# A second buffer for the expert weights that are split into two parts, with the static order of all engines planned anew

## The reference, cut to what matters

```python
xn = _layernorm(x)
# attention: q, k, v = silu(conv4(xn @ W)); delta rule in chunks of 32 steps:
#   att = (I + strict_lower(kb @ k.T))^-1 ; u = att @ v ; w = att @ kb
#   per chunk: u_adj = u - w @ S ; o = q @ S + local @ u_adj ; S += k.T @ u_adj
#   o = gated mix(short FIR, long FIR, o, v) ; rmsnorm ; @ W_o
# experts: top 2 of 8, for each chosen expert e (H=128, F=256):
x1 = xn @ W1[e] + b1[e];  x2 = xn @ W2[e] + b2[e];  z = x1 * x2
g = z @ Wg[e] + bg[e];    l = z @ Wl[e] + bl[e]
y = (silu(g) * l) @ W3[e] + b3[e];   out += weight * y
```

## Time and profile before

| | |
|---|---|
| median of 3 runs (lowest to highest) | 886.43 us (883.74 to 887.36) |
| the profiled execution | 884.17 us, its span 882.4 us |
| busy: PE, DVE, POOL, ACT | 658.0, 568.8, 458.6, 299.6 us |
| mean granted TensorE clock | 0.842 |
| moved by DMA | 64.92 MB, 74 GB/s in the mean |

### The profile page before, as it was taken

The page is one execution under the profiler, slowest core; times in us unless marked ns, Lnnn a source line. Parts: engine busy times, 40 slices in busy tenths (PEclk is TensorE's granted clock), DMA queues, the critical chain, the costliest instruction groups (busy, mean ns, idle before and its releaser), DMA issues.

```text
span 882.4 us, 31011 instructions
## 1 busy us (share of the span) xinstructions
PE 658.0 (75%) x13276; PEld 502.2 (57%) x13276; DVE 568.8 (64%) x1233; ACT 299.6 (34%) x519; POOL 458.6 (52%) x519
## 2 busy tenths in 40 slices
PE   2434856877687878878898686978878788899772
PEld 2223845666465656566666555666566646676651
DVE  6888957536747865965577546864477748533573
ACT  2221024323343425342254334333433343334230
POOL 3730168634826754676475755387435662723323
PEclk9985567989887968997899898898889798999775
DMA  7221121323113214131332204131324311310350
GB/s 290 107 96 54 61 54 39 105 64 86 26 39 78 64 32 114 39 77 53 88 108 64 77 14 108 44 92 38 54 61 74 69 38 45 93 53 31 107 196 12
DMA packets 62488, 64.92 MB, mean 74 GB/s; under 512 B 39824, under 2 KB 47888, under 8 KB 62224
## 3 DMA queue, kind: packets, MB, share of 16 engines
q1 hardware_dynamic: 54880, 46.84, 17.8%
q0 software_dynamic: 5888, 12.07, 6.1%
q10 hardware_dynamic: 1584, 4.04, 1.2%
HBM read 45.35 MB, written 17.56 MB: 71 GB/s over the span
## 4 chain that ended last, share of the span: by engine, by line
PE 29%; issue 21%; POOL 20%; DVE 18%; DMA 6%; ACT 3%; SPq 3%; DVEq 0%; POOLq 0%; ACTq 0%
PE ps_shared L1629 5%; PE ps_shared L1850 4%; POOL y_d L1042 4%; POOL xs L1031 3%; PE ps_g L1625 3%; PE ps_l L1625 3%; PE ps_x L1625 3%; DVE acc L1392 3%; PE ps_shared L1767 3%; POOL sumsq L996 2%; SPq L881 2%; DMA system_d<-masked 2%; DVE solve_prod L1466 2%; PE ps_shared L1625 2%; POOL ssq_o L1068 2%
## 5 line engine op out<-in xcount | busy, mean ns | idle before, releaser
L1042 POOL DMA_INDIRECT y_d<-work,put_i x92 | 92.3, 1004 | 80.5 <-DVE work L1605 57.4
L1031 POOL DMA_INDIRECT xs<-xn_d,owner_i x92 | 94.7, 1030 | 60.2 <-issue 24.6
L1625 PE MATMUL ps_x<-xr,w_up 128*128 128x512 f32 x276 | 98.4, 476 | 17.9 <-issue 12.0
L1076 POOL TENSOR_TENSOR z<-work,z 128x512 fp32r<-128x512 f32 x46 | 60.4, 1314 | 59.5 <-ACT z L1246 59.3
L1625 PE MATMUL ps_g<-z,w_mid 128*128 128x512 f32 x276 | 83.2, 441 | 4.6 <-POOL z L1076 4.2
L1625 PE MATMUL ps_l<-z,w_mid 128*128 128x512 f32 x276 | 82.2, 436 | 1.7 <-issue 1.1
L1392 DVE SCALAR_TENSOR_TENSOR acc<-pre,late_sb,acc 128x512 f32<-128x512 f32 x72 | 59.9, 832 | 26.9 <-ACT acc L1139 25.6
L1625 PEld LDWEIGHTS ps_x<-xr,w_up 128*128 128x128 f32 x276 | 54.8, 218 | 36.5 <-issue 18.9
L1850 PE MATMUL ps_shared<-w_plain,work 128*128 128x128 f32 x368 | 58.2, 323 | 18.1 <-DVE work L1600 13.3
L1466 DVE TENSOR_TENSOR solve_prod<-solve_T,solve_L 128x1 f32<-128x1 f32 (+14 forms) x120 | 49.4, 412 | 28.7 <-DMA solve_L<-system_d 25.3
L1850 PEld LDWEIGHTS ps_shared<-w_plain,work 128*128 128x128 f32 x368 | 53.9, 232 | 22.6 <-issue 16.5
(11 more groups left out here) (252 smaller groups left out, 1420.7 us busy)
## 6 DMA issues: line engine op xcount, KB each, us to landing
w_split<-expert_split SPq DMA_DIRECT2D x23, 768.0 KB
w_plain<-expert_plain SPq DMA_DIRECT2D x23, 196.0 KB
xa_d<-xr SPq DMA_DIRECT2D x8, 512.0 KB, 2.6
xa<-xa_d SPq DMA_DIRECT2D x8, 512.0 KB, 4.0
system_d<-masked SPq DMA_DIRECT2D x8, 256.0 KB, 2.9
x_res<-hidden SPq DMA_DIRECT2D x8, 256.0 KB, 2.8
xs<-xn_d,owner_i POOLq DMA_INDIRECT x92
y_d<-work,put_i POOLq DMA_INDIRECT x92
```

Source lines behind the costliest of these rows:

```text
L1031: pool.indirect_dma_start(xs[par][:, c, :], None, xn_d.rearrange("w p (c d) -> (w p c) d", c=CPW), bass.IndirectOffsetOnAxis(owner_i[:, w ...
L1042: pool.indirect_dma_start(y_d, bass.IndirectOffsetOnAxis(put_i[:, w * CPW + c:w * CPW + c + 1], 0), y_sb[par][:, c * D:(c + 1) * D], None) ...
L1076: pool.tensor_tensor(low[:, :], up1[i], high[:, :].bitcast(FP), ALU.subtract).then_inc(S["z_low"], 1)
L1625: made = pe.matmul(to, weights[a], x[b], start=start and n == 0, stop=stop and n == 2)
```

## The change

1. `w_split` becomes a list of two buffers, used by the tile's parity. `load_split` of tile t waits for the splits of tile t-2, and the landing is counted on one semaphore per buffer (`in_split0`, `in_split1`).
2. The planner's stream `expert_weights` becomes two, one per parity, with the same rule.
3. The descriptor part of SBUF is set to 8 KB per partition, which frees 8 KB; the second buffer takes 6 KB.
4. `PULL` and `LEAN` get other values for many of their names, so all five queues stand in another order. The instructions themselves are the same: 23 loads of 768 KB, the same splits, products and table loads.

```diff
-PULL = {"beta_T": -200, "blend": -600, "choose": 400, "combine": -250, "conv0": 50, "count": -200, "delta_T": 50,
+PULL = {"blend": -600, "choose": 400, "combine": -250, "conv0": 50, "count": -200, "delta_T": 50, "delta_again": 350,
...
-    def expert_weights():
+    def expert_weights(par):
         yield need(("place", 0, 0))
-        for t in range(TILES):
-            if t:
-                yield need(("split_up", t - 1, 0), ("split_mid", t - 1, 0))
+        for t in range(par, TILES, 2):
+            if t >= 2:
+                yield need(("split_up", t - 2, 0), ("split_mid", t - 2, 0))
             yield "load_split", t, 0, None
...
-        w_split = sb("w_split", P, SPLIT)
+        w_split = [sb(f"w_split{n}", P, SPLIT) for n in range(2)]
...
-                    if w:
-                        sp.wait_ge(S["up_low"], w)
-                        sp.wait_ge(S["mid_low"], w)
+                    if w >= 2:
+                        sp.wait_ge(S["up_low"], w - 1)
+                        sp.wait_ge(S["mid_low"], w - 1)
                     row = sp.value_load(row_i[0:1, w:w + 1], min_val=0, max_val=(EXPERTS - 1) * P)
-                    sp.dma_start(w_split[:, :], expert_split[bass.ds(row, P), :]).then_inc(S["in_split"], 16)
+                    sp.dma_start(w_split[par][:, :], expert_split[bass.ds(row, P), :]).then_inc(S[f"in_split{par}"], 16)
...
-                    act.wait_ge(S["in_split"], 16 * (w + 1))
+                    act.wait_ge(S[f"in_split{par}"], 16 * loads(w, 2))
...
-    nc = bacc.Bacc("TRN2", target_bir_lowering=False, num_devices=1)
+    nc = bacc.Bacc("TRN2", target_bir_lowering=False, num_devices=1, dynamic_dma_scratch_size=8192)
```

More of the change, by code:

```diff
@@ L122 @@
-LEAN = {"beta": -30, "beta_T": 45, "blend": 45, "combine": -15, "conv": -30, "delta_again": -40, "fetch": -10,
[L123 to L129, removed]
+PULL = {"blend": -600, "choose": 400, "combine": -250, "conv0": 50, "count": -200, "delta_T": 50, "delta_again": 350,
+        "diag": -100, "down": 200, "fir": -350, "fir_l": -600, "fir_l_T": 600, "fir_l_half": 200, "fir_s_T": -50,
+        "fold": -250, "full": 300, "fuse": -50, "fuse2": -400, "gate": 50, "gate_T": -500, "gates": 300, "gelu": 100,
+        "give": -600, "inv": 100, "inverse_out": 150, "k_T": -600, "ln": -150, "load_split": 200, "load_x": -350,
+        "load_xs": -200, "load_xt": 50, "low": 250, "masks0": -300, "mid_g": 150, "mid_l": -300, "mix_v": -350,
+        "normed": 100, "o": 50, "o_T_out": -100, "on_state": -300, "out": 50, "own": 300, "owned": 600, "place": -200,
+        "products": -250, "project": 250, "q_T": -300, "rank": -150, "solve_in": -200, "solve_mul": -50,
+        "solve_sum": -350, "split": -100, "split_mid": 550, "split_qkv": 300, "split_up": 200, "store": -600,
+        "sumsq": -300, "swish": 300, "system": 500, "times": 50, "turn": -100, "u": -150, "u_adj": 600, "u_out": -150,
+        "up1": -50, "up2": 600, "v_T": -200, "v_again": -150, "w_T_out": 400, "x_res": 150, "y_put": -600, "z": -50,
+        "zeros": 100}
@@ new lines @@
+LEAN = {"beta": -30, "beta_T": 45, "blend": 45, "combine": -15, "conv": -30, "delta_again": -40, "fetch": -10,
+        "fir": -5, "fir_l_T": -25, "fir_s_T": -25, "full": 15, "fuse": -20, "fuse2": 40, "give": -20, "inv": -20,
+        "inverse_out": -20, "k_T": 25, "ln": -40, "load_xs": -5.2, "low": 25, "mark": -15, "masks": -45, "mid_g": 12.1,
+        "mid_l": -15.6, "mix_s": -5, "mix_v": 25, "norm": -35, "o": -15, "o_T_out": -25, "owned": 10, "products": 45,
+        "project": 20, "rank": 30, "rms": -5, "silu": 5, "solve_in": -15, "solve_mul": 30, "split_mid": -13.9,
+        "state": 15, "store": 45, "sumsq": -15, "system": -10, "times": 10.4, "turn": -7.7, "u_adj": 25, "u_out": -15,
+        "up2": -3.4, "v_T": 40, "v_again": -40, "v_again_T": 15, "v_b": -60, "y_out": -8.7, "y_put": -10.4,
+        "zlow": -15.6}
@@ L526, in schedule @@
                windows(triangles), windows(attend), *(expert_loads("load_xs", n, lambda t: ("turn", WINDOWS + t, 0)) for n in range(2)),
-               *(expert_loads("load_plain", n, lambda t: ("y_out", t, 0)) for n in range(2)), expert_weights(),
+               *(expert_loads("load_plain", n, lambda t: ("y_out", t, 0)) for n in range(2)), expert_weights(0), expert_weights(1),
                expert_splits("split_up", 2, "up2"), expert_splits("split_mid", 1, "mid_l"), expert_turns(), expert_ups(), expert_zs(), expert_mids(), expert_gates(), expert_downs(), expert_puts(0), expert_puts(1),
@@ L616 @@
 SIGNALS += [f"in_xa{n}" for n in range(3)]
-SIGNALS += [f"{k}{n}" for k in ("in_xa_d", "in_plain", "in_xs", "in_y_d") for n in range(2)]
+SIGNALS += [f"{k}{n}" for k in ("in_xa_d", "in_split", "in_plain", "in_xs", "in_y_d") for n in range(2)]
 SIGNALS += [f"in_y{n}" for n in range(WINDOWS)]
```

12 lines of the change are left out of this document (6 added, 6 removed).

## The result

The changed kernel takes 901.21 us (median of 3, 898.25 to 905.45) against 886.43: a ratio of 1.0178, 95% interval 1.0104 to 1.0252. Timed again beside later experiments it came out at 1.0121 (1.0066 to 1.0177). So it is slower by 1 to 2%, where the prediction gave 879.7 and a range of 865 to 894. The profiled execution took 905.45 us, 21.3 us of span above the one of before.

The account below looks back on a forecast made before the run. PE's queue was taken to set the pace, its 136 us of standing still being what counts. Pauses -8.54, `down` +5.6, `u_adj` -2.0 and last stage -1.8 gave -6.7: 877.4 profiled, 879.7 us as median, range 865 to 894.

Parts of the forecast that it names:

- Three pauses, -8.54: PE's pauses at window 4's `low`, a window 1 state copy and window 2's `u_out` go: 4.22, 2.05, 2.27 us.
- pause 1: At `low` of window 4, PE stood 4.22 us because `parts` queued behind two `w_split` loads on SP; it goes.
- ACT waits under 10 us, SP's wait far below 245.7: Profile signs: behind 120 us ACT's `w_split` waits total under 10 us; SP's wait for splits far under 245.7.
- `down`, +5.6: PE's wait for DVE's last gate before `down`: nine more short covers at 0.62 us each, +5.6 us.
- The rival that added nine at 2.2: Nine more `down` places cost their mean price, 2.2 us each, 19.8 us together: 893.9 us; chance 0.19.
- The tail, -1.8: Last stage: window 6's `o_T` and `out` leave PE's path to the end; -1.8 us, bounds 0 and -1.8.
- `products` to `low`, 0: PE work covering the triangular solve shrinks in windows 3 and 7, DVE's foreign work too; 0, bounds -5 and +8.
- Descriptors, 0: Smaller descriptor part of SBUF: at most 9 POOL calls in flight, none stretched; 0 us.
- The other sign of being wrong: The prediction would be wrong if PE's idle time between 120 and 830 us did not fall.
- The pauses come back elsewhere: No-change rival: SP's queue still holds loads behind a `w_plain` load waiting for `y_out`; 884 to 888 us, chance 0.24.
- the calls' case: POOL's indirect calls wait for a place in the smaller descriptor ring; chance 0.03.
- the last rival: Order gains more: all 16.4 us of POOL's waits and 4.9 of `u_adj`; 860 us, 868 half way; chance 0.13.

Follow-up runs that it names:

- e6_sp: Kernel before with two w_split buffers, its order kept except in SP's queue: 20 loads of w_split and window 4's parts moved ahead; 1.0029.
- e9_up1: Kernel before with one number of PULL changed that has nothing to do with loads, up1 from 0 to -50; 1.0288.
- e1_ring: Kernel before with only the descriptor ring set to 8 KB; 1.0006.
- e2_buffers: Kernel before with two w_split buffers and the 8 KB ring, every queue in its old order; 1.0035.
- f2: Two buffers; order of the kernel before for 374 of PE's 583 pieces, through tile 14, then the new tables and loads two tiles ahead; 1.0124.
- f3: Two buffers; order of the changed kernel for PE's first 338 pieces, then the old tables with the load one tile ahead; 1.0187.
- e3: Changed kernel with the old tables PULL and LEAN: two buffers, two streams of loads, 8 KB ring; 1.0351.
- f1: Two buffers; order of the kernel before for 140 of PE's 583 pieces, through tile 5, then the new tables and loads two tiles ahead; 1.0362.
- e4: Kernel before with the new tables PULL and LEAN alone: one buffer, one stream of loads, ring as it was; 1.0271.
- e8: Changed kernel, two buffers and two streams, with tables found by a search on the planner's own account; 1.0283.
- e7: Kernel before, one buffer, with tables found by a search on the planner's own account; 1.0048.

## Why the prediction was wrong

- *Three pauses, -8.54.* The step that failed. They were read rightly as to their place and cause, and the change did remove them: 4.22 became 1.01 us, and the other two are gone. But the time did not fall by them, neither here nor in e6_sp, which took their causes away, held the order of PE, DVE, ACT and POOL and came out at 1.0029. The mistake was to treat a pause of PE as time: what PE needed next, from DVE, from ACT or from the instruction queue, was late as well. At pause 1 I took "issue" for the landing of `parts` alone, while 1.89 us of the same group ended 1.5 us behind an instruction packet.
- *ACT waits under 10 us, SP's wait far below 245.7.* Wrong: 27.5 and 275.5. I read from the new order that loads stand a tile ahead, not that their splits had moved ahead with them.
- *`down`, +5.6.* The sum is right, 13.3 us in 6 waits became 18.8 in 15, but the price is luck. I had kept the old waits and added nine at 0.62. In fact three long ones (5.0, 4.0 and 2.7 us) had made up 11.7 of the 13.3, none is over 2.8 now, and the mean of the fifteen is 1.25. The rival that added nine at 2.2 is refuted.
- *`u_adj`, -2.0.* 15.5 to 14.4, inside its bounds. *The tail, -1.8.* From the end of the last `down` to the end of the span it went from 59.0 to 54.0 us, so the tail is shorter, as forecast; but it starts 26 us later.
- *`products` to `low`, 0.* At windows 3 and 7, the two that I had counted, PE has no pause at `parts` now. The 6.48 us came at window 1, which the prediction does not name.
- *Descriptors, 0.* Right (1.0006), but the nine calls in flight were misread. The landings of the earlier trace rows belong to the sixteen loads that read `y_d` back at the end; for a scatter the profile has no landing. From the counts on the semaphores of the gathers and scatters I estimate that the last scatter of a tile landed 2.2 to 4.7 us after its issue, and that four or five calls were in flight at most. No run shows a call that waits for room in this part: with 8 KB the scatters took 1.002 us for 1.004.
- *Everything else about the order, 0.* Together with the first the error that decides. The prediction counts four kinds of cover and takes the others as unchanged. The others cost more: of 15.2 us of new waits for DVE `down` is 5.5, and `mix` on POOL is 4.3 more. e9_up1 shows how little it takes.
- *The clock.* 0.87 to 0.85 between 120 and 830 us, at the edge of what I had allowed. The other sign of being wrong, an idle time there that does not fall, came true: 135.9 became 144.9 us. PE's busy time behind 120 us is 606.1 us for 599.4, but with the order of before it was 604.3 and 606.1 as well (e1_ring, e2_buffers), so I can't put any of the 21.3 us to it with certainty.
- *The rivals.* "The pauses come back elsewhere" described what the buffer alone does, the `w_plain` load that waits for `y_out` included. For the second buffer in the old order e2_buffers and e6_sp measured 1.0035 and 1.0029: the engine that waited for the load, ACT, is busy for a third of the span (299.6 of 882.4 us) and is not the one that sets the pace. No run shows the calls' case, which had 0.03: e1_ring came out at 1.0006. None of the rivals that ended slower was the one that came: a whole new order is a rival by itself, and I gave it no chance. (The half way of the last rival, 868, mixes two bases; between 879.7 and 860 it is 870.)

What stays open: which property of an order makes it good. That the order costs the time is shown: with the old order the descriptor part and the buffer came out at 1.0006 to 1.0035, while the new tables alone, with one buffer, came out at 1.0271. Where it costs it is shown only in part: at the end for f2, f3, e3 and e9, earlier for f1, e4 and e8. The nine other orders (the changed kernel's, e3, e4, e7, e8, e9, f1, f2, f3) were all slower, by 0.5 to 3.6%; the planner's account and the count of covers both failed to say by how much.

## What to carry to other kernels

Before a pause is priced, ask what ends next if it goes, and try it with the order held fixed: the buffer alone in the old queues gained nothing, nor did it with the loads moved ahead. If a change comes with new scheduling constants, the new order is the change; compare it with a few neighbours of the old one before crediting or blaming the feature. And in a kernel with thousands of small products, shift PE's instruction count once or twice with dummy products in a known pause, since that alone moved this one by 1.2%.

## What was not expected of the hardware

PE runs out of instructions, as far as these runs can show it. In before a packet of 16 KB passes about every 126 records of products (105 packets for 13276, and as many of weight loads). The places where PE then stood, for 0.2 to 2.7 us, are mostly those where it had been fast: the 126 products ahead of them had taken 2.6 us in the median, and about 6 at the places of the same raster without a pause. It costs 24 to 46 us of PE's idle time in the kernels above, and the profile shows it only as "issue". It falls where the count of instructions says, not where the work does: 64 or 192 records more moved every such pause to other work, 128 or 256 left 27 and 25 of 34 in place. With the descriptor part at 8 KB per partition instead of 16, the 184 indirect calls of POOL, of which by my estimate no more than five were in flight, took no longer (scatters 1.002 us in the mean for 1.004, the kernel 1.0006).
